# Four-layer graph network on one core: another order of the stages in the hyperbolic loop, and finishing phases cut into pieces

## Chip, cores and metric

The kernel runs on one core of a Trainium2 chip. The metric is the device time of one execution, in microseconds; lower is better.

## What is computed

12,500 nodes with 64 features each and 212,500 edges, sorted by their destination, go through four graph layers. Before each layer the features are normalized over a row and clamped at zero, and each layer's result is added to `x`.

```python
h = relu(layernorm(x)); x = x + L0(h, edge_attr)   # softmax over a node's edges, norm, linear 64->128, batch norm, linear 128->64
h = relu(layernorm(x)); x = x + L1(h)              # mean of the neighbours, linear
h = relu(layernorm(x)); x = x + L2(h)              # hyperbolic attention
h = relu(layernorm(x)); x = x + L3(h, edge_type)   # attention by relation and head
```

The hyperbolic layer computes for every edge a distance between two mapped node rows, turns it with square root, logarithm and exponential into a weight, and sums the weighted rows of each node:

```python
den = 1 + 2*c*duv + c*c*nu*nv
e = -2/sqrt_c * arctanh(clip(sqrt_c * |ma|, 1e-8, CLIP)); att = exp(e) / segment_sum(exp(e))
att_log_h = segment_sum(att * log_h[col]);  z = elu(att_log_h);  h_prime = tanh(norm(z)) * z / norm(z)
```

## The kernel before

The program is a sequence of phases, each a block in which the five engines run their own instruction streams and wait for each other's semaphores. All orders are written by hand. For each layer there is an edge loop (`softmax_edges`, `mean_edges`, `hyperbolic_edges`) and a finishing phase on nodes (`finish_softmax`, `finish_mean`, `finish_hyperbolic`, `finish_relational`). Node tensors lie as 125 partitions x 100 columns (`NB`) x 64 features.

**The hyperbolic loop.** 228 passes (`CHB`), each over eight tiles (`BT`) of 128 edges. The helper `steps(engine, n, (lag, stage), ...)` writes an engine's pass as its stages in the given order; a stage with lag 2 works in pass c on tile group c-2. The first and last passes are written out, and those between are a hardware loop with four passes in its body. The stages are:
- VectorE: `unpack` (the row numbers of the gathers), `differ` (reads `h_ps_src` and the gathered rows, writes `h_diff`), `messages` (gathered rows times weight), `compare` (the one-hot `h_hot`), `distances`, `ratios`, `runs` (running sums of `h_ps_sum`).
- TensorE: `expand` (L1188, `h_ps_src`), `add_up` (L1170, `h_ps_sum`), `turn_hot` (L1179, transposes `h_hot` into `h_ps_hot`).
- ScalarE: `square`, `root`, `move` (L1212, copies `h_ps_hot` to `h_hot_t`), `weigh` (L1216 logarithm, L1219 exponential; the weight), `store` (a DMA issue).
- GpSimd: `gather`, eight indirect DMAs of rows (L1148), which wait for `unpack`. SyncE loads the `h_near` blocks.

`add_up` waits for `messages` of its group and for the `runs` of the group before; `expand` waits for `differ` of the group before and for `move` of its own; `messages` waits for `weigh`; `runs` waits for `add_up`.

**Finishing phases.** Each begins with 100 indirect DMAs on GpSimd's queue, one for each column of nodes, which fetch the last row of a node's running sums (`gather_last`, L1339, or L1888). All of them add to one semaphore, and VectorE waits for all 100 before it works on the whole tensor. In `finish_softmax` the transposes, the first linear layer and its bias (TensorE L1616 and L1624, ScalarE L1643 and L1647) come in 25 groups of 4 columns, then a sum, a square and a root over the whole tensor, one Relu over it (L1654), and 13 groups of the second linear layer (L1631). In `finish_hyperbolic` the linear layer goes column by column through `take`, which copies each result into one of two buffers (`rows_o`, `dst_o`), from which a SyncE DMA and an indirect GpSimd DMA store it. `finish_relational` ends with one DMA of the output.

The edge loops of the other three layers also have eight gathers for each pass on GpSimd's queue: L609 in the two softmax layers and L922 in the mean layer.

Of the kernel before, what the change touches and what calls it, by code (L numbers as in the profile page):

```python
# [72 lines left out]
def build(nc, x, src, dst, edge_attr, edge_type, w0a, b0a, gamma, beta, w0b, b0b, scale0,  # L73
          w1, b1, w2, c2, w3, al3, ar3, b3, out):
    with ExitStack() as whole:
# [59 lines left out]
        def bc(a, width=D):  # L135
            return a[:, :, None].broadcast_to([NP, NB, width])
# [927 lines left out]
        def hyperbolic_edges(c_col, inv_sqrt_c):  # L1064

            with nc.cleanup_on_exit(), ExitStack() as ctx:
# [48 lines left out]
                with nc.Block() as block:  # L1115
# [38 lines left out]
                    def _(pe):  # L1154
# [37 lines left out]
                        steps(pe, CHB, (1, expand), (3, add_up), (0, turn_hot))  # L1192

                    @block.scalar
                    def _(act):
# [31 lines left out]
                        steps(act, CHB, (2, square), (2, root), (0, move), (2, weigh), (3, store))  # L1227
# [107 lines left out]
        def gather_last(pool, into, table, sem):  # L1335
# [7 lines left out]
        GROUPS = NB // GROUP  # L1343

# [64 lines left out]
        def finish_softmax():  # L1409

            with nc.cleanup_on_exit(), ExitStack() as ctx:
# [14 lines left out]
                got_w, gathered, ran, sq_ready, rooted, u_ready, turned, moved, hidden, biased, mean_ready, var_done, \  # L1426
                    std_in, std_out, scaled, relued, z_ready, z_taken, var_ready, std_ready, normed, put, a_step = counter(
                        "n0_got_w n0_gathered n0_ran n0_sq n0_rooted n0_u n0_turned n0_moved n0_hidden n0_biased n0_mean "
# [35 lines left out]
                with nc.Block() as block:  # L1464
# [19 lines left out]
                    def _(pool):  # L1484
# [11 lines left out]
                        pool.wait_ge(gathered, 16 * NB)  # L1496

                    @block.vector
                    def _(dve):
# [68 lines left out]
                        step(v.scalar_tensor_tensor(G[:, :, D:P], G[:, :, D:P], 1e-7, bc(has_edge[:, :]), ALU.add, ALU.mult))  # L1568
                        step(v.tensor_tensor(T[:, :, :], G[:, :, D:P], G[:, :, D:P], ALU.mult))
                        step(v.reduce_sum(m2, T[:, :, :], AX))  # L1570
                        dve.sem_inc(sq_ready, 1)
                        dve.wait_ge(rooted, 1)
                        dve.wait_ge(got_w, 16 * 7)
                        step(v.tensor_scalar(m2, m2, 1e-12, None, ALU.max))
                        step(v.reciprocal(inv, m2))
                        step(v.tensor_tensor(inv, inv, f2, ALU.mult))
                        step(v.tensor_scalar(inv, inv, scale_c[:, :], None, ALU.mult))
                        step(v.tensor_tensor(T[:, :, :], G[:, :, D:P], bc(inv), ALU.mult))
                        step(v.tensor_tensor(T[:, :, :], T[:, :, :], Hn[:, :, :], ALU.add))
                        dve.sem_inc(u_ready, 1)  # L1580
# [23 lines left out]
                    def _(pe):  # L1604
# [4 lines left out]
                        pe.wait_ge(u_ready, 1)  # L1609
# [16 lines left out]
                        pe.wait_ge(relued, 1)  # L1626
                        for g, (z0, z1) in enumerate(zgroups):
                            if g >= 2:
                                pe.wait_ge(z_taken, g - 1)
# [6 lines left out]
                    def _(act):  # L1636
                        a = nc.scalar
                        act.wait_ge(sq_ready, 1)
                        a.activation(small[:, 0:2, :], small[:, 0:2, :], ACT.Sqrt).then_inc(rooted, 1)
                        for g in range(GROUPS + 1):  # L1640
                            if g < GROUPS:
# [383 lines left out]
```

## Time and profile before

| | us |
|---|---|
| runs of the kernel | 11425.31, 11441.29, 11446.05 (median 11441.29) |
| the profiled execution's own time | 11452.29 |
| its span, first to last instruction | 11450.6 |
| softmax edge loop, layer 0 | about 281 to 2433 |
| `finish_softmax` | 2452 to 2930 |
| mean edge loop and `finish_mean` | 2930 to 5634 |
| hyperbolic loop | 5653 (first gather) to 8388 |
| `finish_hyperbolic` | 8393 to 8990 |
| relational edge loop | 8990 to 11187 |
| `finish_relational` | 11195 to 11450.6 |

The profile is one execution. Its time lies 11 us above the median of the three runs. Each phase ends with a barrier, so the phases add up.

### The profile page before, as it was taken

The page shows a single profiled execution, that of the slowest core. Times are in us where ns is not written, and L with a number is a line of the kernel's source. Part 1 is how long each engine was busy: PE and PEld are TensorE (multiplying, and loading weights), DVE is VectorE, ACT ScalarE, POOL GpSimd, SP SyncE. Part 2 cuts the span into 40 slices and gives each one's busy share as a digit, 9 for nine tenths or more (in the row PEclk, how much of TensorE's full clock was granted, in tenths as well). Part 3 has the DMA queues.
Part 4 walks back from the last instruction along what each step waited for, and adds up shares of the span by engine and source line. Part 5 has one row for each costly group of instructions (what it writes and reads, how often), then busy time and mean ns, then how long its engine had stood idle before and what let it go on. Part 6 is the DMA issues. An engine that isn't in the chain of part 4 may idle for free. (4 is left out here: it accounts for less than half of the span.)

```text
span 11450.6 us, 134539 instructions
## 1 busy us (share of the span) xinstructions
PE 6752.2 (59%) x28079; PEld 5273.3 (46%) x28079; DVE 7082.5 (62%) x14431; ACT 4031.5 (35%) x8105; POOL 7668.6 (67%) x7662
## 2 busy tenths in 40 slices
PE   0777777733156666533277777777616677677660
PEld 0444444422045555533177777777613344444440
DVE  3666666663466666624466666666524588888882
ACT  0222222211057666731155555555410133333330
POOL 5777777761577777778666666666542577777774
PEclk9655566555578888865555555555555565555655
DMA  2444444440433333320344444444722344444441
GB/s 79 122 129 129 129 129 129 129 76 7 149 66 67 67 67 66 67 47 8 57 93 91 92 91 92 92 91 91 74 29 70 104 130 128 128 130 127 130 123 40
DMA packets 1419449, 1048.80 MB, mean 92 GB/s; under 512 B 921421, under 2 KB 1138032, under 8 KB 1418781
## 3 DMA queue, kind: packets, MB, share of 16 engines
q0 software_dynamic: 261824, 317.67, 17.5%
q1 hardware_dynamic: 762140, 367.42, 12.9%
q10 hardware_dynamic: 395317, 361.81, 9.8%
q8 instruction: 63, 1.03, 0.0%
q14 instruction: 105, 0.86, 0.0%
HBM read 576.48 MB, written 468.86 MB: 91 GB/s over the span
## 5 line engine op out<-in xcount | busy, mean ns | idle before, releaser
L1148 POOL DMA_INDIRECT h_rows_d<-table,h_idx_s x1824 | 1746.3, 957 | 976.3 <-issue 522.6
L609 POOL DMA_INDIRECT rows<-table3s,idx x1664 | 1648.2, 991 | 517.6 <-issue 501.5
L609 POOL DMA_INDIRECT rows<-table,idx x1664 | 1622.1, 975 | 550.0 <-issue 506.4
L922 POOL DMA_INDIRECT m_rows<-table,m_idx x1664 | 1571.5, 944 | 536.0 <-issue 500.6
L953 PE MATMUL m_ps_sort<-m_hot_high,m_hot_low 128*128 128x216 f32 x3328 | 920.4, 449 | 605.9 <-DVE m_hot_high L1047 532.8
L1188 PE MATMUL h_ps_src<-h_near,h_hot_t 128*128 128x65 f32 x3648 | 827.4, 418 | 722.8 <-DVE h_diff L1286 662.8
L1188 PEld LDWEIGHTS h_ps_src<-h_near,h_hot_t 128*128 128x128 f32 x3648 | 791.0, 329 | 807.5 <-issue 807.5
L953 PEld LDWEIGHTS m_ps_sort<-m_hot_high,m_hot_low 128*128 128x128 f32 x3328 | 825.2, 257 | 675.5 <-DVE m_hot_high L1047 567.1
L725 PE MATMUL ps_score<-ident,rows 128*128 128x128 f32 x1664 | 655.0, 497 | 572.4 <-DMA rows<-table,idx 568.0
L757 PE MATMUL ps_out<-ident,sums 128*128 128x128 f32 x3328 | 715.4, 384 | 286.5 <-DVE sums L680 286.5
L1170 PE MATMUL h_ps_sum<-h_rows_d,h_hot 128*128 128x65 f32 x3648 | 824.8, 417 | 13.2 <-DVE h_rows_d L1312 13.2
L757 PEld LDWEIGHTS ps_out<-ident,sums 128*128 128x128 f32 x3328 | 627.3, 222 | 423.6 <-DVE sums L680 280.2
L1170 PEld LDWEIGHTS h_ps_sum<-h_rows_d,h_hot 128*128 128x128 f32 x3648 | 805.3, 333 | 13.7 <-issue 13.7
L1321 DVE SCALAR_TENSOR_TENSOR h_run<-h_run,h_goes_on,h_ps_sum 128x65 f32<-128x65 f32 x1824 | 514.4, 282 | 468.9 <-PE h_ps_sum L1170 260.6
L1016 DVE TENSOR_TENSOR_SCAN m_sums<-m_same_b,m_sums,m_ps_rows 128x512 f32<-128x512 bf16 x208 | 266.2, 1280 | 868.7 <-issue 671.6
L725 PEld LDWEIGHTS ps_score<-ident,rows 128*128 128x128 f32 x1664 | 416.7, 311 | 831.4 <-issue 831.4
L785 ACT ACTIVATE ps_score<-ps_score 128x512 f32<-128x512 f32 x208 | 121.1, 582 | 1654.8 <-PE ps_score L727 1654.8
L774 ACT ACTIVATE wide<-rows 128x256 f32<-128x256 f32 x416 | 150.0, 407 | 1521.5 <-DMA rows<-table3s,idx 1521.5
L991 ACT ACTIVATE m_hot_low<-m_hot_low,record,m_slope 128x128 f32<-128x128 f32 x1664 | 660.0, 480 | 6.1
L628 DVE TENSOR_TENSOR hot<-bins,cat 128x784 bf16<-128x784 bf16 x208 | 202.9, 976 | 647.6 <-PE ps_count L713 647.6
L1055 DVE SCALAR_TENSOR_TENSOR m_junk<-cat,m_ps_base 128x98 f32<-128x98 f32 (+61 forms) x1664 | 586.9, 420 | 0.0
L727 PE MATMUL ps_score<-ident,attr 128*64 128x128 f32 x3328 | 578.3, 448 | 0.0
(420 smaller groups left out, 14858.5 us busy)
## 6 DMA issues: line engine op xcount, KB each, us to landing
scan<-out_e ACTq DMA_DIRECT2D x832, 256.0 KB
h_near<-table SPq DMA_DIRECT2D x1824, 32.5 KB
run_g<-h_run ACTq DMA_DIRECT2D x228, 260.0 KB
part_b<-part SPq DMA_DIRECT2D x832, 64.0 KB
max_b<-top ACTq DMA_DIRECT2D x416, 128.0 KB, 2.4
scan<-m_out_e SPq DMA_DIRECT2D x416, 128.0 KB
attr<-in_edge_attr SPq DMA_DIRECT2D x415, 128.0 KB
h_rows_d<-table,h_idx_s POOLq DMA_INDIRECT x1824
```

Of the source, the lines that this page charges most:

```text
L609: pool.indirect_dma_start(out=rows[:, b, k, h * GW:(h + 1) * GW], out_offset=None, in_=table3s.rearrange("n (q f) -> (n q) f", f=HEADS) if ...
L725: nc.tensor.matmul(ps_score[:, b % 2, k::TILES], rows[:, b, k, :], ident[:, :], start=True, stop=False)
L727: mm = nc.tensor.matmul(ps_score[h * D:(h + 1) * D, b % 2, k::TILES], attr[:, b, h, k, :], ident[:, :], start=False, stop=True)
L757: mm = nc.tensor.transpose(ps_out[:, j, k * P:(k + 1) * P], sums[:, b % 2, j, k::TILES], ident[:, :])
L922: pool.indirect_dma_start(out=rows[:, b, k, h * D:(h + 1) * D], out_offset=None, in_=table1, in_offset=bass.IndirectOffsetOnAxis(ap=idx[:, ...
L953: nc.tensor.matmul(ps_sort[:, 0:SORTED], hot_low[:, w % 2, j, :], hot_high[:, w % 2, j, :], start=n == 0, stop=n == PC - 1).then_inc(place ...
L991: ins = a.activation(hot_low[:, w % 2, j, :], hot_low[:, w % 2, j, :], ACT.Relu, bias=record[:, at:at + 1], scale=slope[:, at:at + 1])
L1055: v.scalar_tensor_tensor(junk[:, at % 4, 0:BLOCKS + n], cat[:, p, 0:BLOCKS + n], cat[:, p, BLOCKS + n:BLOCKS + n + 1], ps_base[:, 0:BLOCKS ...
L1148: pool.indirect_dma_start(out=rows_d[:, b, k, :], out_offset=None, in_=table2, in_offset=bass.IndirectOffsetOnAxis(ap=idx_s[:, b, k:k + 1] ...
L1170: mm = nc.tensor.matmul(ps_sum[:, k // HB, (k % HB) * ACC2:(k % HB + 1) * ACC2], hot[:, b, k, :], rows_d[:, b, k, D + 1:ROW2], start=True, ...
L1188: mm = nc.tensor.matmul(ps_src[:, k // HB, (k % HB) * (D + 1):(k % HB + 1) * (D + 1)], hot_t[:, b % 2, k * P:(k + 1) * P], near[:, b, k, : ...
L1321: v.scalar_tensor_tensor(run[:, b, k, :], before, goes_on[:, bass.ds(c * BT + k, 1)], ps_sum[:, k // HB, (k % HB) * ACC2:(k % HB + 1) * AC ...
```

## The change

**Hyperbolic loop.** TensorE's pass becomes `add_up`, `expand`, `turn_hot`, and on ScalarE `weigh` now stands ahead of `move`. **finish_softmax** and **finish_relational** work in fifths of 20 columns, each with a semaphore of its own for its 20 gathers; the output goes out in five DMAs; the batch norm's sum is taken from the bias instructions' own accumulators; the Relu is cut into 13 pieces; the addition of `b2row` moves ahead of the wait for the gathers. **finish_hyperbolic** works in quarters of 25 columns up to the norm, and `take` has four buffers in place of two. `gather_last` takes a list of semaphores.

```diff
-                        steps(pe, CHB, (1, expand), (3, add_up), (0, turn_hot))
+                        steps(pe, CHB, (3, add_up), (1, expand), (0, turn_hot))
-                        steps(act, CHB, (2, square), (2, root), (0, move), (2, weigh), (3, store))
+                        steps(act, CHB, (2, square), (2, root), (2, weigh), (0, move), (3, store))
...
-                                        in_offset=bass.IndirectOffsetOnAxis(ap=last_edge[:, b:b + 1], axis=0)).then_inc(sem, 16)
+                                        in_offset=bass.IndirectOffsetOnAxis(ap=last_edge[:, b:b + 1], axis=0)) \
+                    .then_inc(sems[b * len(sems) // NB], 16)
+        DEEP = 4
+        QUARTERS = 4
+        FIFTHS = 5
+        FIFTH = NB // FIFTHS
...
-                        dve.wait_ge(gathered, 16 * NB)
-                        step(v.reciprocal(G[:, :, 0:D], G[:, :, 0:D]))
-                        step(v.tensor_tensor(G[:, :, D:P], G[:, :, D:P], G[:, :, 0:D], ALU.mult))
...
+                        step(v.tensor_tensor(X[:, :, :], X[:, :, :], b2row[:, None, :].broadcast_to([NP, NB, D]), ALU.add))
+                        for q in range(FIFTHS):
+                            at = fifth(q)
+                            dve.wait_ge(gathered[q], 16 * FIFTH)
+                            den, msg, t = G[:, at, 0:D], G[:, at, D:P], T[:, at, :]
+                            wide = [NP, FIFTH, D]
+                            step(v.reciprocal(den, den))
+                            step(v.tensor_tensor(msg, msg, den, ALU.mult))
+                            step(v.scalar_tensor_tensor(msg, msg, 1e-7, has_edge[:, at][:, :, None].broadcast_to(wide), ALU.add, ALU.mult))
+                            step(v.tensor_tensor(t, msg, msg, ALU.mult))
+                            step(v.reduce_sum(m2[:, at], t, AX))
+                            dve.sem_inc(sq_ready, 1)
+                            dve.wait_ge(rooted, q + 1)
...
+                            step(v.tensor_tensor(t, msg, inv[:, at][:, :, None].broadcast_to(wide), ALU.mult))
+                            step(v.tensor_tensor(t, t, Hn[:, at, :], ALU.add))
+                            dve.sem_inc(u_ready, 1)
...
-                        step(v.reduce_sum(mean, Y, AX))
+                        step(v.reduce_sum(mean, y_sums[:, :], AX))
...
+                                if g % (GROUPS // FIFTHS) == 0:
+                                    pe.wait_ge(u_ready, g * FIFTHS // GROUPS + 1)
...
-                                             bias=cols[:, 0:1]).then_inc(biased, 1)
+                                             bias=cols[:, 0:1], accum_out=y_sums[:, h:h + 1]).then_inc(biased, 1)
...
-                        a.activation(Y, Y, ACT.Relu, bias=cols[:, 6:7], scale=cols[:, 5:6]).then_inc(relued, 1)
+                        for z0, z1 in zgroups:
+                            a.activation(Y[:, z0 * NP:z1 * NP], Y[:, z0 * NP:z1 * NP], ACT.Relu, bias=cols[:, 6:7],
+                                         scale=cols[:, 5:6]).then_inc(relued, 1)
...
-                            if g >= 2:
-                                dve.wait_ge(put[g % 2], 16 * (g // 2))
-                                dve.wait_ge(put_v[g % 2], 16 * (g // 2))
+                            if g >= DEEP:
+                                dve.wait_ge(put[g % DEEP], 16 * (g // DEEP))
+                                dve.wait_ge(put_v[g % DEEP], 16 * (g // DEEP))
...
-                        sp.wait_ge(done, 1)
-                        sp.dma_start(nodes(out), X[:, :, :]).then_inc(put, 16)
+                        for q in range(FIFTHS):
+                            sp.wait_ge(done, q + 1)
+                            sp.dma_start(nodes(out)[:, fifth(q), :], X[:, fifth(q), :]).then_inc(put, 16)
```

TensorE in the hyperbolic loop, the first passes of the block, as one piece of the difference (L1179 is `turn_hot`, L1188 `expand`, L1170 `add_up`):

```order
 L1188 MATMUL h_ps_src<-h_near,h_hot_t 128x65 x8
 L1179 MATMUL h_ps_hot<-ident,h_hot 128x128 x8
+L1170 MATMUL h_ps_sum<-h_rows_d,h_hot 128x65 x8
 L1188 MATMUL h_ps_src<-h_near,h_hot_t 128x65 x8
+L1179 MATMUL h_ps_hot<-ident,h_hot 128x128 x8
 L1170 MATMUL h_ps_sum<-h_rows_d,h_hot 128x65 x8
```

`add_up` now stands directly behind `turn_hot` and ahead of `expand` in every pass.

ScalarE in the same loop, the first pass that has a `root` (L1207), as one piece of the difference (L1216 and L1219 are `weigh`, L1212 is `move`):

```order
 L1207 ACT_TABLE_LOAD
 L1207 ACTIVATE h_ratio<-h_ratio 128x8
+L1216 ACT_TABLE_LOAD
+L1216 ACTIVATE h_ratio<-h_ratio 128x8
+L1219 ACT_TABLE_LOAD
+L1219 ACTIVATE h_weight<-h_ratio,c_cols 128x8
 L1212 ACTIVATE h_hot_t<-h_ps_hot 128x1024
-L1216 ACT_TABLE_LOAD
-L1216 ACTIVATE h_ratio<-h_ratio 128x8
-L1219 ACT_TABLE_LOAD
-L1219 ACTIVATE h_weight<-h_ratio,c_cols 128x8
```

The logarithm and the exponential move ahead of the copy of the transposed one-hot; the number of table loads in a pass stays three.

VectorE in `finish_softmax` of the changed kernel, one fifth, of which five stand one behind the other:

```order
L1585 RECIPROCAL big<-big 125x20x64
L1586 TENSOR_TENSOR big<-big 125x20x64
L1587 SCALAR_TENSOR_TENSOR big<-big,has_edge 125x20x64
L1588 TENSOR_TENSOR T<-big 125x1280
L1589 TENSOR_REDUCE small<-T 125x20
L1592 TENSOR_SCALAR small<-small 125x20
L1593 RECIPROCAL small<-small 125x20
L1594 TENSOR_TENSOR small<-small 125x20
L1595 TENSOR_SCALAR small<-small,scale_c 125x20
L1596 TENSOR_TENSOR T<-big,small 125x1280
L1597 TENSOR_TENSOR T<-T,Hn 125x1280
```

Before, each of these stood once and over all 100 columns.

## Rows read from the trace of the kernel before

**Rows 1.** The profile's page: the span
```profile
span 11450.6 us, 134539 instructions
```

**Rows 2.** Timeline of one hyperbolic pass: start us, us, engine, line, work, idle before and releaser
```profile
7001.62 0.70 DVE L1312 TENSOR_TENSOR h_rows_d<-h_rows_d,h_weight 128x520 f32<-128x520 f32 x1 [1.68 <-ACT h_weight L1219]
...
7003.49 3.62 PE L1170 MATMUL h_ps_sum<-h_rows_d,h_hot 128*128 128x65 f32 x16
...
7006.90 1.91 PE L1179 MATMUL h_ps_hot<-ident,h_hot 128*128 128x128 f32 x8
7007.34 3.19 DVE L1321 SCALAR_TENSOR_TENSOR h_run<-h_run,h_goes_on,h_ps_sum 128x65 f32<-128x65 f32 x8 [0.78 <-PE h_ps_sum L1170]
...
7008.85 1.02 ACT L1212 ACTIVATE h_hot_t<-h_ps_hot 128x1024 f32<-128x1024 f32 x1 [3.58 <-PE h_ps_hot L1179]
...
7010.83 0.68 DVE L1286 TENSOR_TENSOR h_diff<-h_ps_src,h_rows_d 128x512 f32<-128x512 f32 x1
...
7011.58 0.94 POOL L1148 DMA_INDIRECT h_rows_d<-table,h_idx_s  x1 [1.76 <-DVE h_idx_s L1270]
...
7011.61 3.65 PE L1188 MATMUL h_ps_src<-h_near,h_hot_t 128*128 128x65 f32 x16 [2.80 <-DVE h_diff L1286]
...
7012.76 0.30 ACT L1219 ACTIVATE h_weight<-h_ratio,c_cols 128x8 f32<-128x8 f32 x1
```

**Rows 3.** Sums by window, `differ` alone, 2450 us of the hyperbolic loop
```profile
5728.00:8178.00 2450.00, 143.36 (x211) 0.51 0.50 91
```

**Rows 4.** Gathers of three edge loops by line: count, busy, mean ns, idle, releasers
```profile
L1148 POOL DMA_INDIRECT h_rows_d<-table,h_idx_s x1731 | 1657.9, 958 | 860.9 <-issue 497.0 <-DVE h_idx_s L1270 363.9
L609 POOL DMA_INDIRECT rows<-table3s,idx x1653 | 1637.2, 990 | 503.7 <-issue 498.5 <-DMA idx<-src 3.3 <-PE ps_mult L749 1.8
L922 POOL DMA_INDIRECT m_rows<-table,m_idx x1613 | 1523.1, 944 | 518.3 <-issue 485.7 <-DMA m_idx<-src_g 32.6
```

**Rows 5.** Sums by window, the last 160 us of the hyperbolic loop, all engines
```profile
8220.00:8380.00 160.00, 74.63 (x340) 71.30 (x340) 65.51 (x216) 57.60 (x75) 53.27 (x56) 0.50 0.85 56
```

**Rows 6.** Timeline of `finish_softmax` and, for its bias instructions, first and last start
```profile
2627.80 40.15 DVE L1566 RECIPROCAL big<-big 125x6400 f32<-125x6400 f32 x1 [81.56 <-DMA big<-scan,last_edge]
...
2711.34 1.87 PE L1616 MATMUL n_ps_t<-ident,T 125*64 125x125 f32 x8 [257.26 <-DVEq L1580]
...
L1647 ACT ACTIVATE big<-n_ps_y,cols x25: 677/677/678, 2715.2 to 2784.3; 128x500 f32<-128x500 f32 x25
...
2785.12 13.17 DVE L1585 TENSOR_REDUCE cols<-big 128x1 f32<-128x12500 f32 x1 [66.93 <-ACT big L1647]
...
2810.57 10.80 ACT L1654 ACTIVATE big<-big,cols 128x12500 f32<-128x12500 f32 x1 [0.87 <-DVEq L1593]
```

**Rows 7.** Timeline of finishing phases: gathers beside wide VectorE instructions
```profile
2459.59 6.82 DVE L1505 TENSOR_REDUCE small<-T 125x100 f32<-125x6400 f32 x1
...
2462.49 1.21 POOL L1339 DMA_INDIRECT big<-scan,last_edge  x1 [0.30 <-issue]
...
11197.52 6.83 DVE L1984 TENSOR_TENSOR X<-X,b_row 125x6400 f32<-125x6400 f32 x1 [11.62 <-DMA b_row<-in_L_gnn_h_bias]
...
11198.70 6.73 POOL L1339 DMA_INDIRECT G<-scan,last_edge  x1 [0.30 <-issue]
```

**Rows 8.** Timeline of `finish_hyperbolic`, VectorE: the first and the last instruction up to the norm
```profile
8553.19 0.25 DVE L1922 TENSOR_SCALAR s2s<-acc_s 125x100 f32<-125x100 f32 x1 [165.52 <-DMA acc_s<-run_g,final_row]
...
8587.63 6.82 DVE L1689 TENSOR_REDUCE s2s<-T 125x100 f32<-125x6400 f32 x1
```

**Rows 9.** `take` in `finish_hyperbolic`: first and last start, its second start, its waits
```profile
L1956 DVE COPY rows_o<-lin_ps_y x100: 757/758/759, 8658.3 to 8980.9; 125x576 f32<-125x576 f32 x100
...
8660.98 0.76 DVE L1956 COPY rows_o<-lin_ps_y 125x576 f32<-125x576 f32 x1 [1.68 <-PE lin_ps_y L1380]
...
  DMA at_first<-dst_o,first_row: 212.8, 94
```

**Rows 10.** Timeline of `finish_relational`: VectorE behind the gathers, SyncE's output DMA
```profile
11360.08 3.50 DVE L1986 TENSOR_SCALAR G<-G 125x6400 f32<-125x6400 f32 x1 [155.74 <-DMA G<-scan,last_edge]
...
11424.43 0.27 SPq L1971 DMA_DIRECT2D out<-X  x1
```

More of the change, by code:

```diff
@@ L1333, in scatter_runs, with gather_last, fifth, quarter @@
                                             in_=in_runs[:, g, k * RUN:(k + 1) * RUN], in_offset=None).then_inc(sem, 16)
-        def gather_last(pool, into, table, sem):
+        def gather_last(pool, into, table, sems):
             for b in range(NB):
                 pool.indirect_dma_start(out=into[:, b, :], out_offset=None, in_=table,
-                                        in_offset=bass.IndirectOffsetOnAxis(ap=last_edge[:, b:b + 1], axis=0)).then_inc(sem, 16)
+                                        in_offset=bass.IndirectOffsetOnAxis(ap=last_edge[:, b:b + 1], axis=0)) \
+                    .then_inc(sems[b * len(sems) // NB], 16)
         GROUP = 4
         GROUPS = NB // GROUP
+        DEEP = 4
+        QUARTERS = 4
+        FIFTHS = 5
+        FIFTH = NB // FIFTHS
+        def fifth(q):
+            return slice(q * FIFTH, (q + 1) * FIFTH)
+        def quarter(q):
+            return slice(q * (NB // QUARTERS), (q + 1) * (NB // QUARTERS))
         class Linear:
@@ L1608, in _ @@
                         mm.then_inc(prefixed, 1)
-                        pe.wait_ge(u_ready, 1)
                         pe.wait_ge(got_w, 16 * 7)
@@ L1905, in _ @@
                         a = nc.scalar
-                        act.wait_ge(ask_exp, 1)
-                        a.activation(T[:, :, :], T[:, :, :], ACT.Exp).then_inc(exped, 1)
+                        for q in range(QUARTERS):
+                            act.wait_ge(ask_exp, q + 1)
+                            at = quarter(q)
+                            a.activation(T[:, at, :], T[:, at, :], ACT.Exp).then_inc(exped, 1)
                         act.wait_ge(ask_root, 1)
@@ L1976, in _ @@
                         gather_last(pool, G, scan3, gathered)
-                        pool.wait_ge(gathered, 16 * NB)
+                        for q in range(FIFTHS):
+                            pool.wait_ge(gathered[q], 16 * FIFTH)
                     @block.vector
@@ L1984, in _ @@
                         step(v.tensor_tensor(X[:, :, :], X[:, :, :], b_row[:, None, :].broadcast_to([NP, NB, D]), ALU.add))
-                        dve.wait_ge(gathered, 16 * NB)
-                        step(v.tensor_scalar(G[:, :, 0:D], G[:, :, 0:D], 1e-16, None, ALU.max))
-                        step(v.reciprocal(G[:, :, 0:D], G[:, :, 0:D]))
-                        step(v.tensor_tensor(G[:, :, D:2 * D], G[:, :, D:2 * D], G[:, :, 0:D], ALU.mult))
-                        step(v.tensor_tensor(G[:, :, D:2 * D], G[:, :, D:2 * D], bc(has_edge[:, :]), ALU.mult))
-                        step(v.tensor_tensor(X[:, :, :], X[:, :, :], G[:, :, D:2 * D], ALU.add))
-                        dve.sem_inc(done, 1)
+                        for q in range(FIFTHS):
+                            at = fifth(q)
+                            dve.wait_ge(gathered[q], 16 * FIFTH)
+                            den, msg = G[:, at, 0:D], G[:, at, D:2 * D]
+                            step(v.tensor_scalar(den, den, 1e-16, None, ALU.max))
+                            step(v.reciprocal(den, den))
+                            step(v.tensor_tensor(msg, msg, den, ALU.mult))
+                            step(v.tensor_tensor(msg, msg, has_edge[:, at][:, :, None].broadcast_to([NP, FIFTH, D]), ALU.mult))
+                            step(v.tensor_tensor(X[:, at, :], X[:, at, :], msg, ALU.add))
+                            dve.sem_inc(done, 1)
         softmax_edges(0)
```

100 lines of the change are left out of this document (52 added, 48 removed).

## The prediction

> **What bounds the kernel now.** I first cut the span [rows 1] into its phases: each ends with a barrier, so a phase is worth what its own last wait is worth, and the whole-span busy shares say nothing about this change. Three kinds of place matter.
>
> *The hyperbolic loop.* The view by windows counts 211 starts of `differ` in 2450 us, so a pass takes 2450/210 = 11.67 us [rows 3]. The timeline of one pass [rows 2] shows why. TensorE runs `expand`, `add_up` and `turn_hot` back to back, then stands 2.80 us until `differ` releases the next `expand`. `differ` is late because VectorE ran `runs` first, and `runs` waits for `add_up`, which stands behind `expand`. So one ring sets the pass: `expand` (3.4 us from its start to `add_up`'s), `add_up` 3.7, 0.2 to VectorE, `runs` 3.2, `unpack` and `differ` about 1.0, together 11.5. The reader is to see also that `messages` waits 1.68 us for the weight, which ScalarE makes only after `move`, and that GpSimd stands 1.76 us waiting for `unpack`.
>
> *The waits for 100 gathers.* VectorE stands 81.6 us in `finish_softmax`, 165.5 in `finish_hyperbolic` and 155.7 in `finish_relational` [rows 6, 8, 10], and all its work comes behind the last gather.
>
> *`take`.* 99 steps from 8658.3 to 8980.9 are 3.26 us each; 94 of them wait for the store out of the buffer, 212.8 us in all [rows 9].
>
> **The hyperbolic loop changed.** With `add_up` ahead of `expand`, `runs` can start while `expand` runs; nothing is added, three table loads stay three. What is the next bound? Four candidates, all from [rows 2]:
> - TensorE alone: 3.3 + 3.4 + 2.1, and no wait between: 8.8 us.
> - VectorE alone: the pass of 11.57 less its two waits (1.6 for the weight, 0.8 for `runs`): 9.2 us.
> - A ring over two passes: `messages` ends, `add_up` and `expand` 6.7, `turn_hot` 2.1, `move` 1.0, `store`'s issue and `square` 1.1, then on VectorE `distances`, `ratios` 3.1, `runs` 3.2, `unpack` and `differ` 1.0, `messages` 0.7, handovers 0.4: 19.3 us, or 9.7 a pass.
> - GpSimd: eight gathers at 0.958 us and 0.30 between them [rows 2, 4]: 10.06 us.
>
> So GpSimd's queue becomes the bound and TensorE no longer is. Its pace in practice: the mean layer's loop pays (1523.1 + 518.3)/1613 x 8 = 10.13 us a pass, the relational one 10.36 [rows 4]. The ends are 10.0 (0.94 + 0.30) and 10.36; I take 10.2, nearest to the mean loop with a little for VectorE's one instruction with two SBUF operands (`messages`), of which more below. Gain: (11.67 - 10.2) x 210 = **309 us** (274 to 350). The last 160 us of the loop run at a DMA share of 0.85 with TensorE under half busy [rows 5]; there transfers, not the order, set the pace, and I count nothing. If the moved `move` or `weigh` lost this cover, each 0.1 us of a pass would cost 21 us.
>
> **The added work beside the gathers** needs a price first. A gather that starts inside a wide two-operand VectorE instruction takes 6.73 us in place of 1.21, until just behind that instruction's end at 11204.35; one that starts inside a wide reduction takes 1.21 [rows 7]. GpSimd's queue is in order, so such a delay moves every later gather. Cut in pieces, the two-operand instructions of 1.4 us come in short bursts beside the gathers of 1.5 us pitch. Bounds: nothing, up to their whole length. I take one part-delay per burst: 2 us a fifth, 3 us a quarter. The wide reciprocal beside a gather is nowhere in the trace; it reads one operand like the reduction, so I take zero, and its price if it blocks is a rival below.
>
> The Trainium skill, "SBUF — State Buffer", section "Who interferes with whom", says the same and speaks against this change: an instruction with two SBUF inputs, or a copy in a two-port mode, locks GpSimd out for its whole length, while one with at most one SBUF input outside those modes does not. The 6.73 us gather agrees. Read as the full length of every such instruction, `finish_softmax` would gain 20 us less than below; by the page the reciprocal costs nothing.
>
> **finish_softmax.** From the last landing (2627.8) to the sum (2785.1) are 157.3 us [rows 6]. Behind the last fifth's landing remain: reciprocal 40.15/5 = 8.0, five two-operand instructions and a reduction 6 x 1.4, small ones and the root 1.4, so 17.8; then 5 of 25 groups on TensorE at 2.9 us ((2784.3 - 2715.2)/24) and a tail, 15.2. That is 33, a gain of 124. The other four fifths must fit before: VectorE is free from 2546, adds `b2row` (6.8), and four fifths at 17.8 plus some 1.7 of waiting for ScalarE (which must finish the fifth before) end near 2631. The gathers are pushed by 6 (`b2row`) and 4 x 2 us, so the last lands near 2642: minus 14 (bounds 6 and 34). The sum over accumulators in place of the whole tensor saves 13.0, the first Relu piece in place of all 9.7; the accumulator reads hide under TensorE's 2.9 us groups. Together 110 + 13 + 10 = **133 us** (112 to 147).
>
> **finish_hyperbolic.** Up to the norm 41.3 us lie behind the landing [rows 8]; a quarter, with a short wait for its exponential, is 11.3. Gain 30, less 3 quarters x 3 = **21 us** (6 to 30). `take` with four buffers: the second step came 2.66 us behind the first, with no buffer to wait for, and was released by TensorE [rows 9]. A store's round trip of two pitches (about 6 us) over four buffers is 1.5, under 2.66. 99 x 0.60 = 59; some late stores remain: **55 us** (30 to 59).
>
> **finish_relational.** From the landing to the end of the span are 11450.6 - 11360.1 = 90.5 us, of which the output DMA takes 26.2 [rows 1, 10]. Behind the last fifth: 0.8 + 8.0 + 3 x 1.4 + gaps = 13.2, and a fifth of the output, between 5.2 and twice that; I take 7. Gain 70, less 4 x 2 of pushed gathers: **62 us** (50 to 70).
>
> **Sum.** 309 + 133 + 21 + 55 + 62 = 580. The profiled execution's own time is 11452.3, so 10872; the median of the runs is 11.0 lower, so **10861 us**. All terms at their good ends (656) give 10785, all at their poor ends (472) 10969.
>
> **Rivals.**
> - *The ring, not the gathers, sets the pass.* For: my 9.7 leaves 0.4 us, and ScalarE's order makes `square` wait behind `move` and `store`. Against: the ring's durations are all in one pass. At 10.9 the loop gains 162: 11008.
> - *The wide reciprocal blocks gathers.* For: it is long and not seen. Against: the reduction. Each of four fifths pushes its gathers by some 7.3 us in two phases: 58 lost, 10919.
> - *The swap does nothing for the loop*, because a wait of the same length (a landing of `h_near`, `h_rows_d`) stands behind it: 11.67 stays, 11170. Against: no such wait appears in the pass.
> - *Slower.* `expand` now stands behind `add_up`, which waits for `messages` and so for the weight. If the weight still came behind `move`, the ring would be `move` to exponential 4.2 (8.85 to 13.06), `messages` 0.8, `add_up`, `expand` 6.7, `turn_hot` 2.1: 13.8 us a pass, 756 us above the forecast, 11617. It decides once the weight lands later than about 2 us behind `turn_hot`; the new ScalarE order puts it ahead of `move`, so it should not.
>
> **Chances.** Forecast 73%, ring 12%, reciprocal 8%, no effect of the swap 5%, slower 2%. The forecast's own range is 10785 to 10969. 10785 to 10985 holds it nearly, the reciprocal case and a part of the ring case: about 8 in 10. A measurement can tell 0.2% (23 us) from no change; faster 0.97, same 0.01, slower 0.02.
>
> **What would show it.** Loop: starts of `differ` 10.2 us apart, GpSimd's wait for `unpack` gone, and TensorE and VectorE each with a wait that was not there. `finish_softmax`: the first transposes before the last gather, the sum gone, the z groups starting 1 us behind the scale. Gathers of over 2 us beside `b2row` and beside bursts, none inside a reciprocal. `take`: pitch 2.7, released by TensorE. Output: five DMAs, the last over within some 7 us. It would be wrong if the pass stands at 10.7 or more, or if the gathers of a finishing phase end 30 us later than before.

## The result and the profile after

The changed kernel takes 10830.81 us (median of four, 10824.22 to 10834.15), the kernel before 11439.4 beside it; the ratio is 0.9468 (95% interval 0.9454 to 0.9482). The forecast was 10861, the range 10785 to 10985. The profiled execution spans 10832.4 us, 618.2 less than before. Cut at the same marks in both traces, the terms are:

| | forecast, us less | in the two traces |
|---|---|---|
| hyperbolic loop, 210 passes | 309 | 322.4 |
| its last passes | 0 | 16.2 |
| `finish_softmax` | 133 | 140 |
| `finish_hyperbolic` up to the norm | 21 | 23.5 |
| `take` and what follows it | 55 | 41.8 |
| `finish_relational` | 62 | 73.4 |

The small rest lies in the phases that the change doesn't touch. First the loop. The view by windows of `differ` alone, from its 7th start to its 217th (stretch, length, VectorE's busy time, its count, granted clock, DMA share, GB/s):

```profile
5589.70:7718.00 2128.30, 143.78 (x211) 0.51 0.56 105
```

2127.3 us between the first and the last start are 10.13 a pass; [rows 3] gave 11.67. GpSimd's gathers in this stretch, by line:

```profile
L1148 POOL DMA_INDIRECT h_rows_d<-table,h_idx_s x1688 | 1614.3, 956 | 514.7 <-issue 511.0 <-DVE h_idx_s L1270 3.7
```

(1614.3 + 514.7)/1688 x 8 = 10.09 us for eight gathers, and the wait for `unpack`, 363.9 us before [rows 4], is 3.7. One pass on the timeline, where [rows 2] showed the old one:

```profile
6401.57 3.62 PE L1188 MATMUL h_ps_src<-h_near,h_hot_t 128*128 128x65 f32 x16
...
6402.11 3.19 DVE L1321 SCALAR_TENSOR_TENSOR h_run<-h_run,h_goes_on,h_ps_sum 128x65 f32<-128x65 f32 x8
...
6403.67 0.30 ACT L1219 ACTIVATE h_weight<-h_ratio,c_cols 128x8 f32<-128x8 f32 x1
...
6406.54 0.17 DVE L1284 TENSOR_TENSOR h_prod<-h_ps_src,h_rows_d 128x8 f32<-128x8 f32 x1 [1.08 <-DMA h_rows_d<-table,h_idx_s]
...
6406.93 1.02 ACT L1212 ACTIVATE h_hot_t<-h_ps_hot 128x1024 f32<-128x1024 f32 x1 [2.96 <-PE h_ps_hot L1179]
6407.22 0.69 DVE L1312 TENSOR_TENSOR h_rows_d<-h_rows_d,h_weight 128x520 f32<-128x520 f32 x1
...
6408.15 3.65 PE L1170 MATMUL h_ps_sum<-h_rows_d,h_hot 128*128 128x65 f32 x16 [1.26 <-DVE h_rows_d L1312]
```

`runs` lies beside `expand`, the weight is ready 3.3 us before `messages`, and what VectorE waits for is the landing of gathered rows (216.6 us in the 210 passes, more than for anything else).

`finish_softmax`, VectorE's last fifth and the sum, and GpSimd's gathers at the two places that matter:

```profile
2548.96 6.83 DVE L1579 TENSOR_TENSOR X<-X,b2row 125x6400 f32<-125x6400 f32 x1
2555.82 8.15 DVE L1585 RECIPROCAL big<-big 125x1280 f32<-125x1280 f32 x1
...
2633.31 8.15 DVE L1585 RECIPROCAL big<-big 125x1280 f32<-125x1280 f32 x1
...
2648.98 0.18 DVE L1592 TENSOR_SCALAR small<-small 125x20 f32<-125x20 f32 x1 [1.41 <-ACT small L1661]
...
2670.36 0.18 DVE L1602 TENSOR_REDUCE cols<-y_sums 128x1 f32<-128x25 f32 x1 [17.35 <-ACT big L1667]
```

```profile
2550.31 6.56 POOL L1338 DMA_INDIRECT big<-scan,last_edge  x1 [0.30 <-issue]
...
2564.74 1.84 POOL L1338 DMA_INDIRECT big<-scan,last_edge  x1 [0.30 <-issue]
...
2624.55 1.22 POOL L1338 DMA_INDIRECT big<-scan,last_edge  x1 [0.30 <-issue]
```

The last gather has ended on GpSimd by 2625.8, so its rows are there near 2628, an estimate (in the trace of before VectorE was released 2.2 us behind that gather's end); VectorE takes them up at 2633.3. It ran without a wait for rows from the end of `b2row` on. The sum, 13.17 us in [rows 6], is 0.18.

`take` (durations, first and last start; what it waited for); then, for `finish_relational`, VectorE's last fifth on the timeline, and the output DMAs by line:

```profile
L1985 DVE COPY rows_o<-lin_ps_y x100: 756/758/759, 8158.4 to 8435.9; 125x576 f32<-125x576 f32 x100
...
  DMA table3s<-rows_o: 138.2, 75
  PE lin_ps_y L1390: 45.3, 25
```

```profile
10811.11 0.83 DVE L2021 TENSOR_SCALAR G<-G 125x1280 f32<-125x1280 f32 x1 [16.94 <-DMA G<-scan,last_edge]
```

```profile
L2002 SPq DMA_DIRECT2D out<-X x5: 262/263/274, 10702.5 to 10824.8; - x5
```

The pitch of `take` is 277.5/99 = 2.80 us. Behind the landing of the last gathered rows come 21.3 us in place of 90.5.

One thing the forecast did not see. GpSimd's waits during the 100 gathers of `finish_hyperbolic`, before and after (total, count, longest):

```profile
POOL acc_s L1888 <- issue: 35.0, 99, 2.7
```

```profile
POOL acc_s L1910 <- issue: 30.2, 99, 0.3
```

In the trace of before every such phase has two stands, pauses of GpSimd for which the profile shows no cause, of 2.7 to 3.1 us, behind the 39th and the 78th gather (in `finish_softmax` the first is 9.5 us). After the change they are left only in the prologue and `finish_mean`, whose gathers still share one semaphore.

### The profile page after: what moved, and what is told of

It is laid out like the page before. It is cut to its first block and busy times, and to the rows that moved or that the text cites. A ratio compares the mean times of both kernels' runs of the same rounds, so it can differ in the third digit from the quotient of the medians.

```text
span 10832.4 us, 134717 instructions
## 1 busy us (share of the span) xinstructions
PE 6721.5 (62%) x28079; PEld 5256.1 (49%) x28079; DVE 7065.2 (65%) x14522; ACT 4045.0 (37%) x8149; POOL 7686.2 (71%) x7662
## 5 line engine op out<-in xcount | busy, mean ns | idle before, releaser
L1170 PE MATMUL h_ps_sum<-h_rows_d,h_hot 128*128 128x65 f32 x3648 | 816.4, 414 | 380.0 <-DVE h_rows_d L1312 380.0
L1170 PEld LDWEIGHTS h_ps_sum<-h_rows_d,h_hot 128*128 128x128 f32 x3648 | 780.5, 325 | 464.1 <-issue 464.1
L1188 PE MATMUL h_ps_src<-h_near,h_hot_t 128*128 128x65 f32 x3648 | 823.4, 417 | 27.0 <-DMA h_near<-table 22.4
L1188 PEld LDWEIGHTS h_ps_src<-h_near,h_hot_t 128*128 128x128 f32 x3648 | 803.3, 332 | 28.2 <-issue 28.2
```

What stands on the lines that cost most here:

```text
L1170: mm = nc.tensor.matmul(ps_sum[:, k // HB, (k % HB) * ACC2:(k % HB + 1) * ACC2], hot[:, b, k, :], rows_d[:, b, k, D + 1:ROW2], start=True, ...
L1188: mm = nc.tensor.matmul(ps_src[:, k // HB, (k % HB) * (D + 1):(k % HB + 1) * (D + 1)], hot_t[:, b % 2, k * P:(k + 1) * P], near[:, b, k, : ...
```

## Experiments

The first four ran on a chip on which the kernel before itself took 14303.96 us. The expectations below explain this by register instructions of the sequencers that come 0.7 us apart. The traces bear that out in part only. Of SyncE's `FUSED_REGOPS` at L1131, mostly 0.06 or 0.15 us each and never over 0.5 us in the trace of before, 3 to 19% took over 0.5 us in these four traces; but SyncE still issues its loads of `h_near` 41 to 50 us (median) ahead of the `expand` that reads them, so the loop does not wait for SyncE, and the register instructions of VectorE, ScalarE and GpSimd take what they took. What is late are the handovers. ScalarE's `move`, which follows the end of `turn_hot` by 0.04 us in the trace of before, follows it by a median of 2.7 us in `e4_sems_only`; one of them (TensorE ends at 8004.50):

```profile
8002.59 1.91 PE L1179 MATMUL h_ps_hot<-ident,h_hot 128*128 128x128 f32 x8
...
8007.46 1.02 ACT L1212 ACTIVATE h_hot_t<-h_ps_hot 128x1024 f32<-128x1024 f32 x1 [8.20 <-DMA scan<-out_e]
```

Why they are late is open. The ratios of these runs say nothing of the two rings; three of them were run again elsewhere. The single gathers and wide instructions took nearly what they take here (a gather 0.96 to 0.99 us on average, 0.96 in the trace of before; `differ` 0.68 in all).

**TensorE's order alone.**

```diff
-                        steps(pe, CHB, (1, expand), (3, add_up), (0, turn_hot))
+                        steps(pe, CHB, (3, add_up), (1, expand), (0, turn_hot))
```

> The kernel before with TensorE's new order alone (add_up, expand, turn_hot); ScalarE keeps move ahead of weigh. My theory, the ring of the prediction's slow rival: the weight comes 4.2 us behind the start of move, then messages 0.8, add_up and expand 6.7, turn_hot 2.1, 13.8 us a pass instead of 11.67; over some 216 passes 460 us more, 11900 us (11800 to 11950), VectorE's wait for the weight and TensorE's wait for messages both over 4 us a pass. Rival: TensorE's order alone frees runs and brings most of the gain, and ScalarE's order only trims it: pass 10.2 to 11, total 11120 to 11300.

Measured there: 14652.2 us, ratio 1.0266 (1.0235 to 1.0297), pass 16.06, against 14.7 with the old orders (in the trace of `e4_sems_only`, which keeps them).

> The kernel before with TensorE's new order alone, run again where register instructions should stand at 0.15 us. Theory, the prediction's slow rival: the ring is move to exponential 4.2, messages 0.8, add_up and expand 6.7, turn_hot 2.1, 13.8 us a pass; total 11900 (11800 to 11950), slower by 3 to 4%. Rival: TensorE's order alone brings most of the gain: pass 10.2 to 11, total 11120 to 11300.

Measured: 11949.43 us beside 11441.08, ratio 1.0445 (1.0428 to 1.0463). Pass 14.0 us. VectorE's waits in 210 passes:

```profile
DVE h_rows_d L1312 <- ACT h_weight L1219: 997.9, 210, 5.0
```

4.75 us a pass for the weight: the slow ring, forecast at 13.8. With TensorE's order alone the kernel is 4.5% slower.

**ScalarE's order alone.**

```diff
-                        steps(act, CHB, (2, square), (2, root), (0, move), (2, weigh), (3, store))
+                        steps(act, CHB, (2, square), (2, root), (2, weigh), (0, move), (3, store))
```

> The kernel before with ScalarE's new order alone (weigh ahead of move). Theory: the ring expand, add_up, runs, differ holds neither weigh nor move as long as both are done within TensorE's wait, so the pass stays at 11.67 us and the total within 0.2% of 11440; only VectorE's wait for the weight (1.68 us) vanishes and the one for add_up grows by as much. Rival: move comes later behind the two table loads and expand waits for it: a pass of 12.5 or more, 11620 or more.

Measured there: 14170.89 us, ratio 0.9914 (0.9891 to 0.9937), pass 13.96. On that chip the weight's earlier place goes with 0.9% less time; why, no run shows.

> The kernel before with ScalarE's new order alone, run again where register instructions should stand at 0.15 us. Theory: the ring expand, add_up, runs, unpack, differ holds neither weigh nor move, so the pass stays at 11.67 us and the total within 0.2% of before; VectorE's wait for the weight goes and its wait for add_up grows by as much. Rival: move comes later and expand waits for it, a pass of 12.5 or more and a total over 11600.

Measured: 11444.02 us beside 11445.63, ratio 1.0001 (0.9991 to 1.001), pass 11.66. The wait moved and nothing was won:

```profile
DVE h_run L1321 <- PE h_ps_sum L1170: 553.5, 210, 2.8
```

Before, the same stretch had 317.8 us of waiting for the weight and 208.5 for `add_up`, 526 together.

**Both orders, nothing else.** Both edits above.

> The kernel before with both new orders in the hyperbolic loop and nothing else of the change. Theory: the parts add up, so this one holds the loop's share of the measured 608 us: pass 10.13, total 11440 less 322 and less 16 in the last passes, 11102 us (11090 to 11120). Rival: part of what the loop seems to give in the full change comes from elsewhere (the queue's state, the clock), total over 11130.

Measured there: 14607.15 us, ratio 1.0209 (1.0179 to 1.024), pass 15.96 and irregular (10.7 to 21.9 us in the 210 passes, 8.6 to 22.8 among the first). On that chip the part of the change that gains most here made the kernel 2% slower. The whole change was not run there.

> The kernel before with both new orders in the hyperbolic loop alone, run again. In the last call the kernel before itself took 14304 us in place of 11440, and the traces show why: in the loops the sequencers' own register instructions, 0.15 us each in the trace of before, came 0.7 us apart, so every engine was short of instructions and the passes irregular (8.6 to 22.8 us); that says nothing of the two rings. If here the register instructions stand at 0.15 us: pass 10.13, total 11440 less 322 and 16, 11102 us (11090 to 11120). Rival as before: over 11130. If they stand at 0.7 us again: slower than before by about 2%, as in the last call, because the new order leaves less slack for an engine whose instructions are late.

Measured: 11136.75 us beside 11455.23, ratio 0.9726 (0.971 to 0.9742), 318 us less; pass 10.16. The total lies 35 us above the 11102 expected, outside my band and, to the letter, in the rival's (over 11130). 15 of the 35 lie in the kernel before, which was that much above its usual median too. The other 20 are gain that did not come (318 for 338): 7 in the 210 passes, and most of the rest in the last passes, so the 16 us there do not belong to the order.

**The pieces alone.** The changed kernel with the two lines put back.

> The changed kernel with both orders of the hyperbolic loop put back: the finishing phases in pieces alone. Theory: the two halves of the change add up, since a barrier lies between them: before less changed is 608, of which the loop alone gave 314 to 318, so this one gives 290 to 294: about 11150 (11135 to 11165), pass 11.67. Rival: the halves share a gain or pay each other (GpSimd's queue state at the loop's end), and this one is off that by over 20 us.

Measured: 11157.37 us beside 11437.9, ratio 0.9749 (0.9734 to 0.9764), 281 us less (290 to 294 expected), pass 11.66. 318 + 281 = 599 against 609: the halves add up within the spread of the runs.

**Is GpSimd's queue the loop's new bound? A ninth gather.**

```diff
+                            pool.indirect_dma_start(
+                                out=spare_rows[:, b, :], out_offset=None, in_=table2,
+                                in_offset=bass.IndirectOffsetOnAxis(ap=idx_s[:, b, 0:1], axis=0)).then_inc(got_rows[b], 16)
```

> The changed kernel with a ninth gather in every hyperbolic pass: it fetches the first tile's rows once more into a buffer that nobody reads, and differ waits for it too. Theory: GpSimd's queue of gathers sets the changed loop's pass (8 x (0.95 + 0.30) + 0.1 = 10.13), so one more gather adds its whole length: 11.37 us a pass, 1.24 x 216 = 268 us more, about 11100. Rival: the pass is set by a ring of the other engines that happens to be as long, and GpSimd only follows it by the wait for unpack; then one more gather is hidden in part and the pass stays below 10.9, total below 11000.

Measured: 11134.33 us, 303 above the changed kernel, of two runs; 210 passes in 2398.3 us, 11.42 each:

```profile
5605.00:8003.50 2398.50, 143.19 (x211) 0.51 0.54 99
```

One gather and its pause, 1.25 us, lengthen the pass by 1.29: nothing of it is hidden. 216 passes make 279 of the 303; another 24 lie in the last passes.

**And what comes next? Seven gathers.** This kernel leaves out the rows of every eighth tile, so its output is another.

```diff
-                            for k in range(BT):
+                            for k in range(BT - 1):
```

> The changed kernel with seven gathers in a hyperbolic pass in place of eight: the rows of the eighth tile are not fetched (its buffer holds ones at the start), so the output is another. It asks what the loop would run at without the eighth gather. Theory: the queue is then down to 7 x 1.25 + 0.1 = 8.9 us and the next bound shows, which by my sums is the ring over two passes at 9.7 us (TensorE alone 8.8, VectorE alone 9.2): pass 9.7, total 10830 less 0.43 x 216 = 10740. Rival: the ring is shorter than I counted and VectorE, 9.2 us busy in a pass, sets it: pass 9.2 to 9.4, total 10630 to 10680. Second rival: the queue is not the bound, and the pass stays above 10.0.

Measured: 10665.8 us, of two runs; pass 9.39. The first rival holds: my ring of 9.7 was counted too long. VectorE's waits in 187 passes:

```profile
DVE h_ratio L1306 <- ACT h_ratio L1207: 51.4, 187, 0.3
DVE h_dist L1295 <- ACT h_diff L1203: 50.5, 93, 0.7
DVE h_idx_s L1272 <- issue: 22.3, 47, 0.5
DVE h_prod L1286 <- issue: 7.2, 47, 0.2
```

131 us, 0.7 a pass, three quarters of it for short answers of ScalarE and none for TensorE or for gathered rows; the rest of 9.4 is VectorE's own work, 7.4 us busy, and the short pauses between its instructions. TensorE, busy for 8.5 us of the pass, waits for `messages`. So behind the queue stands VectorE's chain, only 0.7 us away.

**The stands behind the 39th gather.** The kernel before; only which semaphore a gather adds to is changed, nobody's work comes earlier.

```diff
-                                        in_offset=bass.IndirectOffsetOnAxis(ap=last_edge[:, b:b + 1], axis=0)).then_inc(sem, 16)
+                                        in_offset=bass.IndirectOffsetOnAxis(ap=last_edge[:, b:b + 1], axis=0)).then_inc(sem[b % len(sem) if len(sem) == 4 else b * len(sem) // NB], 16)
...
-                        dve.wait_ge(gathered, 16 * NB)
+                        for q, one in enumerate(gathered):
+                            dve.wait_ge(one, 16 * NB // len(gathered))
```

> The kernel before; the 100 gathers of each finishing phase add to several semaphores, but every waiting engine still waits for all of them, so no work comes earlier. In the trace of before GpSimd stands 2.7 to 3.1 us (once 9.5) behind the 39th and the 78th gather of every finishing phase; in the changed kernel these stands are gone in the three phases whose gathers are split and there in the one whose gathers are not. Arms: finish_softmax five semaphores of 20 gathers in turn, finish_mean two of 50, finish_hyperbolic three of 34, 33 and 33, finish_relational four that take turns at every gather. Theory: GpSimd stands once a semaphore has 39 gathers that nobody has waited for; so none in finish_softmax, finish_hyperbolic and finish_relational, and in finish_mean one behind the 39th and one behind the 89th. Total 11440 less 9, 5 and 6, about 11420. Rival 1: the stand belongs to the number of gathers in the queue, whatever their semaphore; then all stay at 39 and 78, and the total with them. Rival 2: it needs 39 in a row; then the same arms as in the theory are free of it, but finish_mean shows it behind the 39th and the 89th only if the count starts anew with the second semaphore, and the fourth arm doesn't tell them apart.

The total can't tell: 14295.43 us, ratio 0.9989 (0.9972 to 1.0006), where 20 us less were expected. The phases themselves do. `finish_mean`, two semaphores of 50, behind its 39th and its 89th gather:

```profile
6406.00 1.21 POOL L1339 DMA_INDIRECT table_s<-scan,last_edge  x1 [0.31 <-issue]
6409.95 1.21 POOL L1339 DMA_INDIRECT table_s<-scan,last_edge  x1 [2.74 <-issue]
```

```profile
6484.10 1.21 POOL L1339 DMA_INDIRECT table_s<-scan,last_edge  x1 [0.30 <-issue]
6487.86 1.21 POOL L1339 DMA_INDIRECT table_s<-scan,last_edge  x1 [2.55 <-issue]
```

`finish_softmax` in this kernel and in the one with both orders, which ran on the same chip with one semaphore:

```profile
L1339 POOL DMA_INDIRECT big<-scan,last_edge x100: 1205/1209/7087, 2983.6 to 3142.6; - x100
```

```profile
L1339 POOL DMA_INDIRECT big<-scan,last_edge x100: 1208/1212/7093, 2980.6 to 3153.1; - x100
```

159.0 against 172.5 us. In `finish_hyperbolic` and in `finish_relational` (four semaphores in turn) the stands are gone as well. So for these gathers the count is kept for each semaphore and starts anew with the next: rival 1 falls. Rival 2, that it takes 39 in a row, is not told apart from the theory, since no semaphore of the four in turn gets more than 25 gathers. Nor is 39 a number for every DMA: `finish_mean`'s 216 scatters on one semaphore have a single stand of 3.0 us, behind the 113th, before and after the change. What GpSimd does in a stand, these runs don't show.

**A version with what the traces point to.** Gathers of the prologue and of `finish_mean` on five semaphores, the prologue's comparison in fifths, ten buffers in `take`, `b_row` in fifths, and:

```diff
-                        step(v.tensor_tensor(X[:, :, :], X[:, :, :], b2row[:, None, :].broadcast_to([NP, NB, D]), ALU.add))
                         for q in range(FIFTHS):
...
                             dve.sem_inc(u_ready, 1)
 
+                        step(v.tensor_tensor(X[:, :, :], X[:, :, :], b2row[:, None, :].broadcast_to([NP, NB, D]), ALU.add))
                         dve.wait_ge(biased, GROUPS)
...
-                        sp.dma_start(nodes(table2[0:N, :])[:, :, D + 2:ROW2], G[:, :, D:2 * D]).then_inc(put, 16)
...
+                        act.wait_ge(tabled, 1)
+                        act.dma_start(nodes(table2[0:N, :])[:, :, D + 2:ROW2], G[:, :, D:2 * D]).then_inc(put, 16)
```

> The changed kernel with what the traces point to. (a) All gathers that still shared one semaphore (the 100 of the prologue and of finish_mean) go to five: 5 to 6 us less in each, and the prologue's comparison and sum work in fifths, 22 us less behind its last gather. (b) finish_softmax: b2row is added behind the last fifth, in VectorE's wait for TensorE, not ahead of the first, where the trace shows VectorE, not the gathers, as the last to be ready: 6 us less (rival: the gathers were what counted, 0 to 1 us). (c) finish_mean: the second table store goes to ScalarE's queue, beside the first on SyncE's; both in one queue took 112 us from 5385 to 5497 at a DMA share of 0.44 while GpSimd's scatters were over at 5457. Theory: two queues share nothing that is full, the stores end by 5450 and the scatters set the phase: 40 us less, and 8 more from (a) and shorter locks (rival: the engines' time, not the queue, sets the stores; then under 10 us). (d) take with ten buffers: pitch 2.80 to 2.67, 12 us less. (e) b_row in finish_mean and finish_relational in fifths: a gather is held to the end of a 1.4 us piece and not of 6.8: 4 us less in the latter. Sum 100, total about 10730; all rivals, 10800.

Measured: 10797.31 us, ratio to before 0.9436 (0.9423 to 0.945), 34 us below the changed kernel and not 100, at the end where I had put all rivals (10800). By phase against the trace of the changed kernel: prologue 19.9 less, `finish_softmax` 6.8, `finish_mean` 10.2, `take` and what follows it 8.2, `finish_relational` 5.4; the hyperbolic loop came out 12.7 longer, 4 of it in the 210 passes. So (a) gave 20 in the prologue for some 27, and (e) 5 in `finish_relational` for 4. (b) held: VectorE, not the gathers, was late. (d) half: the pitch is 2.66, 14 us less over 99 steps, but the next phase's first gather comes only 8 earlier, since the phase waits for its stores to land. (c) fell to its rival. The stores in the changed kernel and here, over the stretch in which both stores run (queue: packets, MB, share of 16 engines):

```profile
q1 hardware_dynamic: 24986, 6.49, 42.3%
```

```profile
q1 hardware_dynamic: 10911, 2.88, 21.3%
q10 hardware_dynamic: 10912, 2.79, 20.8%
```

24986 packets in 111 us are 225 a us; 21823 in 96 us are 227. Two queues share one pace, and a DMA share of 0.44 did not mean that more could be had from a second queue. The Trainium skill, "DMA: Bandwidth & Descriptors", section "Issuing engines are not separate DMA queues", says that DMAs from different engines run on the same 16 DMA engines and interleave; the measurement agrees.

**One store of whole rows.** The last kernel, with the row of `table2` built whole in `G`:

```diff
-                G = sb("G1", [NP, NB, 2 * D], F32, ctx)
+                G = sb("G1", [NP, NB, ROW2], F32, ctx)
...
-                        sp.dma_start(nodes(table2[0:N, :])[:, :, 0:D + 2], table[:, :, :]).then_inc(put, 16)
-                        sp.wait_ge(put, 32)
+                        sp.dma_start(nodes(table2[0:N, :]), G[:, :, :]).then_inc(put, 16)
+                        sp.wait_ge(put, 16)
```

> The last kernel (better) with finish_mean's two table stores made one: the row of table2 (520 bytes) is built whole in one tile, so that each partition's 100 rows go out as one contiguous stretch in place of 100 pieces of 264 and 100 of 256 bytes. In the last kernel two queues moved the pieces no faster than one (222 a us together, as one queue alone), and the phase waited for them for 50 us after the last scatter. Theory: the number of pieces sets the stores, so whole rows take about twice the 26 us that the output's 3.2 MB took in one DMA before, they are over before the scatters, and the phase ends with these: 45 us less than the last kernel, about 10750. Rival: the bytes or the scatters beside it set the pace, and it gains under 10.

Measured: 10760.9 us (10755.9 to 10765.19), ratio to before 0.9403 (0.939 to 0.9416). `finish_mean` is 35.8 us shorter than in the last kernel, where I had expected 45. The store now, in 50 us:

```profile
q1 hardware_dynamic: 125, 6.24, 29.6%
```

125 packets in place of some 25,000, and the same bytes are over before the last scatter. So it was the pieces, not the bytes or the scatters beside them, that set the store's time; one contiguous stretch a partition was worth 36 us. This is the fastest of the kernels that compute everything, 70 us below the changed one.

## Why the prediction was right, and where it was off

*The loop.* Right in mechanism and nearly in size: 10.13 us a pass for a forecast of 10.2, bound by the gathers. The chosen pace was that of the mean layer's loop with 0.07 added for `messages`; nothing had to be added. Three runs carry it: both orders alone give the gain, a ninth gather is paid in full, and TensorE's order alone gives the slow ring at 14.0 (forecast 13.8). The ring over two passes, 9.7, was mis-sized: with one gather less the pass is 9.39, and VectorE sets it. The 16 us of the last passes, which the prediction put at nothing, are not explained by the order: they took 184.5 to 195.6 us in three traces of loops with the old orders, and 179.4 to 191.6 in four with the new ones.

*The price of pieces beside the gathers* was the term that was off. I took one part-delay for each burst, 2 us a fifth and 3 a quarter. In `finish_softmax` the bursts lengthened five gathers by 3.7 us in all, 0.9 a fifth; in `finish_relational` by 0.34 a fifth; in `finish_hyperbolic` by 3.65 a quarter. The timeline of one burst in `finish_relational` shows how the cheap ones get by:

```profile
10697.83 1.21 POOL L1338 DMA_INDIRECT G<-scan,last_edge  x1 [0.30 <-issue]
10697.85 1.50 DVE L2023 TENSOR_TENSOR G<-G 125x1280 f32<-125x1280 f32 x1
10699.35 1.21 POOL L1338 DMA_INDIRECT G<-scan,last_edge  x1 [0.30 <-issue]
10699.39 1.49 DVE L2024 TENSOR_TENSOR G<-G,has_edge 125x1280 f32<-125x1280 f32 x1
10700.86 1.21 POOL L1338 DMA_INDIRECT G<-scan,last_edge  x1 [0.30 <-issue]
```

A gather that started just ahead of the instruction runs on in 1.21 us, and pieces of 1.5 us have the gathers' own pitch, so each gather starts just ahead of the next piece. The whole `b2row`, by contrast, held one gather for 6.56 us. The rule of the Trainium skill that the prediction weighed ("SBUF — State Buffer", section "Who interferes with whom") is borne out for an instruction that is already running when a gather starts. The section also says that whoever issues first holds the shared ports while the other is blocked, which the prediction left out. The cheap gathers fit the first half of it; the second is not seen, since the instruction behind such a gather took 1.50 us for 1.49. Adding up the full length of all such instructions would have charged a fifth 7.5 us in `finish_softmax` (five of 1.5) and 4.5 in `finish_relational` (three), where 0.9 and 0.34 were paid. The reciprocal: 20 gathers started inside it in `finish_softmax` and 20 in `finish_relational`, and none was lengthened (1.22 us at most), so that rival is out.

*What I had not seen* worked the other way: two stands for each phase, 11.9 us in `finish_softmax`, 4.9 and 5.6 in the two others, vanish with the split semaphores. They were in the trace of before, as the longest of GpSimd's waits for "issue"; I had read only the sums. By an estimate from these rows, with the stands left in, the last rows of `finish_softmax` would have landed near 2640, 6 us behind VectorE, and the three phases together would have gained some 17 us less. So of the 37 us by which the terms of the table come out above the forecast's 580, some 17 are the stands and 16 the last passes, neither of which the prediction had.

*finish_softmax.* 140 for 133, by two errors that cancel in part. The last landing, forecast at 2642, was near 2628; but the fifth behind it began at 2633.3, since VectorE was the late one: `b2row` stood at the head of its queue. And what lies behind was 37.1 us, not 33, with ScalarE's root 1.4 us late in each of the last three fifths. The sum (13) and the Relu (9.5 for 10) came as forecast. The good end of this term's range was added up wrongly: with a push of 6, the lower bound given, it is 124 - 6 + 23 = 141 and not 147, which leaves the forecast as it is and moves the lower end of the total from 10785 to 10791.

*finish_hyperbolic up to the norm.* 23.5 for 21. Behind the landing 29.6 us were gained (forecast 30). The gathers became 6.1 us longer and not 9: the bursts cost 10.9, and the stands gave 4.9 back.

*take.* 41.8 for 55. The step that failed is the round trip of a store, taken as 6 us whatever the number of buffers. In the trace of before a waiting step was released 4.7 to 7.5 us behind the issue of the SyncE store out of its buffer (median 5.3); with four buffers it was 8.8 to 12.3 (median 10.1). So 75 of the 100 steps still wait for a store, and the pitch fell to 2.80 and not to 2.66, the pace of TensorE, which ten buffers reach. Why a store takes longer with more of them on their way was not tested. And 3 us are given back behind the last step, where the phase waits for the landings.

*finish_relational.* 73.4 for 62: 69.2 behind the landing (forecast 70), and 4.1 that the gathers became shorter by where I had them 8 longer.

## What to carry to other kernels

Write down the ring for each half of a reordering: here ScalarE's order alone was worth nothing, TensorE's alone cost 4.5%, and both together gave 2.7%. When a loop comes down to the pace of one in-order queue, adding and leaving out one item of that queue tells in two runs that it is the bound and how far the next one is. When a phase is cut into pieces that wait for their own data, look at what stands on the working engine's queue ahead of the first piece, and count packets, not the busy share, before more queues are put on a store.

## What the runs showed of the hardware

- In the rows of 100 gathers GpSimd stands 2.7 to 3.1 us (9.5 once, 10.9 in one trace) behind the 39th gather that adds to one semaphore, and again behind the 78th; with a new semaphore the count starts anew. 216 scatters on one semaphore have one stand, behind the 113th. Why is open.
- A gather that starts inside a VectorE instruction with two SBUF operands ends just behind it (6.56 us and 6.73 in place of 1.21); one that started just ahead of it (0.02 us) takes 1.21, and one inside a reciprocal of 8.15 us at most 1.22.
- Stores in pieces of 256 and 264 bytes go at some 226 packets a us over all 16 DMA engines at a busy share of 0.44, from one queue or from two.
- On one of the chips the kernel before took 25% longer, ScalarE's `move` came a median of 2.7 to 2.9 us late in the loop in two of four traces, and the sign of the loop's gain turned (1.0209 against 0.9726). Why is open.
